# Six local-attention layers on one core: the product with V from a banded probability tile, and small VectorE steps on GpSimd or PSUM

## What is computed

```python
bk2, bv2 = (look(bk), look(bv))                 # previous window and own window
sim = jnp.einsum('bhwie,bhwje->bhwij', bq, bk2) * QK_SCALE
sim = jnp.where(mask, -jnp.finfo(sim.dtype).max, sim)
attn = jax.nn.softmax(sim, -1)
out = jnp.einsum('bhwij,bhwje->bhwie', attn, bv2)
```

## Time and profile before

| | |
|---|---|
| runs | 3551.12 us median, 3550.79 and 3555.56 the others |
| span of the profiled execution | 3553.3 us |
| time of the profiled execution | not listed by itself; one run is above its span, 3555.56 us |
| busy | TensorE 3325.9 us (94%), VectorE 2737.3 (77%), ScalarE 2545.5 (72%), GpSimd 2041.5 (57%) |
| mean granted TensorE clock | 0.984 |

### The profile page before, as it was taken

How to read it: one execution, slowest core, us unless ns; L and a number is a source line. 1 busy time by engine, 2 the same in 40 slices (tenths; PEclk the granted TensorE clock), 3 DMA queues, 4 the chain that set the end, 5 groups by cost and what they waited for, 6 DMA issues and landing times.

```text
span 3553.3 us, 149054 instructions
## 1 busy us (share of the span) xinstructions
PE 3325.9 (94%) x65032; PEld 2107.6 (59%) x65032; DVE 2737.3 (77%) x3420; ACT 2545.5 (72%) x5866; POOL 2041.5 (57%) x1557
## 2 busy tenths in 40 slices
PE   7999987999999999999999999999999999999996
PEld 3444434666666666666666666666666666666663
DVE  3656557888887878888788878788888878788883
ACT  4667655777777777777777767677777777787774
POOL 0000006766676666766666666667676667676661
PEclk9999998999999999999999999999999999999998
DMA  3223224333333333433333333334333333333330
GB/s 109 76 71 84 75 61 141 135 127 127 134 133 133 118 127 130 140 131 129 119 122 136 130 124 127 127 124 143 126 130 126 121 136 125 135 127 131 129 122 24
DMA packets 247337, 423.34 MB, mean 119 GB/s; under 512 B 71966, under 2 KB 110108, under 8 KB 246556
## 3 DMA queue, kind: packets, MB, share of 16 engines
q1 hardware_dynamic: 220368, 397.28, 33.1%
q10 hardware_dynamic: 26316, 16.52, 1.6%
HBM read 124.21 MB, written 7.34 MB: 37 GB/s over the span
## 4 chain that ended last, share of the span: by engine, by line
PE 64%; DVE 17%; issue 7%; ACT 5%; POOL 5%; DMA 1%; SPq 1%; DVEq 0%; POOLq 0%; ACTq 0%
PE PS L535 64%; DVE TPB L932 5%; DVE MX L956 2%; ACT SC L1237 1%; DVE NV L947 1%; POOL K L1324 1%; POOL Q L1342 1%; DMA RB<-root_scratch 1%; POOL K L1342 1%; DVE PP L977 1%; DVE PX L978 1%; DVE NV L945 1%; DVE H L800 1%; DVE H L1000 1%; DVE NV L949 1%
## 5 line engine op out<-in xcount | busy, mean ns | idle before, releaser
L932 DVE SCALAR_TENSOR_TENSOR TPB<-PS,VEC,C 128x1024 f32<-128x1024 f32 x768 | 961.8, 1270 | 102.0 <-ACT SX L1213 95.0
L1237 ACT ACTIVATE SC<-PS,BQ,RQ 128x64 f32<-128x64 f32 x3072 | 979.5, 436 | 40.7 <-DVE BQ L961 40.3
L1213 ACT ACTIVATE SX<-PS 128x512 f32<-128x512 f32 x768 | 461.5, 620 | 391.4 <-PE PS L535 388.4
L1324 POOL TENSOR_TENSOR K<-K,RB 128x512 f32<-128x512 f32 x384 | 497.2, 1295 | 283.1 <-DMA RB<-root_scratch 278.4
L1347 POOL TENSOR_TENSOR SC<-SC,RC 128x1024 f32<-128x1024 f32 x192 | 366.3, 1908 | 480.2 <-DVE RC L969 478.8
L535 PEld LDWEIGHTS PS<-PP,VV 32*64 32x64 f32 x24576 | 433.7, 133 | 278.6 <-issue 276.3
L535 PE MATMUL PS<-PP,VV 32*64 32x64 f32 (+1 forms) x24576 | 541.2, 223 | 7.8 <-issue 6.2
L1342 POOL TENSOR_TENSOR K<-TPB,TR 128x512 f32<-128x512 f32 x384 | 496.4, 1293 | 0.0
L1342 POOL TENSOR_TENSOR Q<-TPB,TR 128x512 f32<-128x512 f32 x384 | 495.5, 1290 | 0.0
L535 PE MATMUL PS<-LXH,LH 128*128 128x512 f32 x768 | 371.3, 484 | 85.2 <-DVE TPB L932 68.4
L535 PE MATMUL PS<-K,Q 64*32 64x64 f32 (+1 forms) x24576 | 302.2, 224 | 49.5 <-issue 48.0
(11 more groups left out here) (167 smaller groups left out, 5809.8 us busy)
## 6 DMA issues: line engine op xcount, KB each, us to landing
TR<-TPB SPq DMA_DIRECT2D x768, 256.0 KB, 2.7
RB<-root_scratch SPq DMA_DIRECT2D x768, 128.0 KB
PP<-PX SPq DMA_DIRECT2D x192, 192.0 KB, 2.6
WS<-in_wqkv ACTq DMA_DIRECT2D x72, 128.0 KB, 2.4
PP<-PX SPq DMA_DIRECT2D x192, 48.0 KB, 2.5
QA<-TH SPq DMA_DIRECT2D x128, 64.0 KB, 2.1
QA<-TL SPq DMA_DIRECT2D x128, 64.0 KB, 2.1
KA<-TH SPq DMA_DIRECT2D x128, 64.0 KB, 2.1
```

The source lines that it names most:

```text
L932: e.scalar_tensor_tensor(TPB[:, n % 3:4 + n % 2:3 + n % 2 - n % 3, w, :], g, VEC[:, l, 9 + w:10 + w], C[:, at:at + 1024].rearrange("p (o c ...
L1213: e.activation(SX[i % 3][:, :], bk("PJ", key)[:, :], ACT.Square).then_inc(sem["pj_act"], 1)
L1237: p = e.activation(SC[m % 2][:, g, :, :].rearrange("p x k -> p (x k)"), bank[s][:, at:at + 64], ACT.Exp, bias=BQ[m % 2][:, g:g + 1], scale ...
L1324: e.tensor_tensor(dst, dst, RB[n % 2][:, :], ALU.mult).then_inc(sem["pr_pool"], 1)
```

## The change

- PV has two rounds of 16 products. Each takes 64 rows (two windows) and moves 96 columns (three output windows); PP has three blocks per row, of which one in each row quarter is zero and never written again. The four products of one c are two row halves by two column halves, and all products of one row half write one bank at a time.
- TT transposes both parts into two PX tiles, and the stage PX fills PP with eight DMAs on SP's queue where there were two.
- NM2 becomes four GpSimd instructions; BQ becomes a GpSimd instruction (a stage of its own), and the maximum is negated as it is taken.
- rsqrt() keeps its intermediate and its result in the PSUM bank of the sums; F3 reads it there. The bank is held until the last reader is done.
- All of PLACE has new numbers.

```diff
-    "LS": 221.000, "LB": -1.200, "LO": -0.800, "S1": -0.074, "MX": 0.116, "S3": (0.544, 0.762, 0.998, 1.143),
-    "SU": 1.382, "NP": 1.294, "TT": 2.458, "PX": 2.427, "PV": (4.410, 5.233, 5.448, 5.789), "PVn": 6.127,
-    "PJ": (-7.620, -7.132), "PQ": (-7.575, -7.217), "PT": (-7.306, -7.188), "TS": -6.939, "SS": -6.491,
-    "AD": -5.748, "NM1": -3.351, "NM2": -3.290, "RW": -3.234, "RQ": -1.711, "RB": -2.631, "PR": -2.007,
-    "XS": -9.372, "XSl": -9.254, "VP": -0.635, "VC": -0.652, "WO": (12.673, 12.742, 12.742, 12.755),
+    "LS": 220.609, "LB": -1.007, "LO": -0.147, "S1": -0.039, "MX": 0.127, "BQ": -0.409,
+    "S3": (0.527, 0.769, 0.988, 0.821), "SU": 1.191, "NP": 1.545, "TT": 2.465, "PX": 2.765, "PV": (4.790, 5.030),
+    "PVn": 6.097, "PJ": (-7.633, -7.092), "PQ": (-7.531, -7.184), "PT": (-7.291, -7.112), "TS": -6.917, "SS": -6.304,
+    "AD": -5.801, "NM1": -3.418, "NM2": -3.856, "RW": -3.141, "RQ": -1.741, "RB": -3.132, "PR": -1.967, "XS": -9.711,
+    "XSl": -10.141, "VP": -0.635, "VC": -0.581, "WO": (12.860, 12.894, 12.955, 12.965), "F1": 13.910, "F2": 14.289,
...
-        lay(z + P["F2"], group, "F2", u, "f2_dve", 3 * u + 1)
+        lay(z + P["F2"], group, "F2", u, "f3_dve", u + 1)
...
-        PP = [sb(f"PP{i}", [128, 2, 16, 32]) for i in range(2)]
-        PX = sb("PX", [128, 16, 32])
+        PP = [sb(f"PP{i}", [128, 3, 16, 32]) for i in range(2)]
+        PX = [sb(f"PX{i}", [128, 16, 32]) for i in range(2)]
...
                 elif st == "PX":
                     m, = key
-                    a, z = PX, PP[m % 2]
+                    z = PP[m % 2]
+                    if m == 0:
+                        on.wait_ge("band_pool", 2)
                     if m > 1:
-                        on.wait_ge("pv_pe", 4 * m - 4)
+                        on.wait_ge("pv_pe", 2 * m - 2)
+                    on.wait_ge("tt_dve", 2 * m + 1)
+                    for r in range(4):
+                        k = slice(32 * r, 32 * r + 32)
+                        e.dma_start(z[k, r % 2, :, :], PX[0][k, :, :]).then_inc(sem[f"px_in{m % 2}"], 16)
                     on.wait_ge("tt_dve", 2 * m + 2)
-                    e.dma_start(z[0:96, 1, :, :], a[32:128, :, :]).then_inc(sem[f"px_in{m % 2}"], 16)
-                    e.dma_start(z[96:128, 1, :, :].rearrange("p (x c) a -> p x c a", c=4)[:, :, 0:3, :],
-                                a[0:32, :, :].rearrange("p (x c) a -> p x c a", c=4)[:, :, 1:4, :]).then_inc(sem[f"px_in{m % 2}"], 16)
+                    for r in range(1, 4):
+                        e.dma_start(z[32 * r - 32:32 * r, 1 + (r + 1) % 2, :, :],
+                                    PX[1][32 * r:32 * r + 32, :, :]).then_inc(sem[f"px_in{m % 2}"], 16)
+                    e.dma_start(z[96:128, 2, :, :].rearrange("p (x c) a -> p x c a", c=4)[:, :, 0:3, :],
+                                PX[1][0:32, :, :].rearrange("p (x c) a -> p x c a", c=4)[:, :, 1:4, :]).then_inc(sem[f"px_in{m % 2}"], 16)
...
                     else:
-                        on.wait_ge("pv_pe", 4 * p + rho)
+                        on.wait_ge("pv_pe", 2 * p + 1)
                     for c in range(4):
-                        for x in range(2):
+                        for t in range(2):
                             for s in range(2):
-                                r = (rho + 2 * x + s) % 4
-                                j = 4 * c + r
-                                w = min(2, 16 - j)
+                                x = (t + rho) % 2
+                                j = 4 * c + 2 * t
+                                w = min(3, 16 - j)
                                 h = 2 * ((2 * p + x) % 8) + s
-                                y = mm(bank[2 + x][64 * s:64 * s + 64, 32 * j:32 * j + 32 * w],
-                                       VV[32 * r:32 * r + 32, c, 64 * h:64 * h + 64],
-                                       PP[p % 2][32 * r:32 * r + 32, 0:w, 8 * s + 4 * x + c, :],
-                                       rho == 0 and c == 0, rho == 3 and c == 3, skip_group_check=True)
+                                k = slice(64 * t, 64 * t + 64)
+                                y = mm(bank[2 + x][64 * s:64 * s + 64, 32 * j:32 * j + 32 * w], VV[k, c, 64 * h:64 * h + 64],
+                                       PP[p % 2][k, 0:w, 8 * s + 4 * x + c, :], rho == 0 and c == 0, rho == 1 and c == 3,
+                                       skip_group_check=True)
...
-            def rsqrt(v, u, x, step, done, r):
+            def rsqrt(v, x, y, step, done, r):
                 on.wait_ge(step, 2 * r + 2)
-                e.scalar_tensor_tensor(u, v, EPS, x, ALU.add, ALU.mult).then_inc(sem[done], 1)
+                e.scalar_tensor_tensor(v, v, EPS, x, ALU.add, ALU.mult).then_inc(sem[done], 1)
                 on.wait_ge(done, 3 * r + 1)
-                e.scalar_tensor_tensor(u, u, -0.5, x, ALU.mult, ALU.mult).then_inc(sem[done], 1)
+                e.scalar_tensor_tensor(v, v, -0.5, x, ALU.mult, ALU.mult).then_inc(sem[done], 1)
                 on.wait_ge(done, 3 * r + 2)
-                e.scalar_tensor_tensor(x, u, 1.5, x, ALU.add, ALU.mult).then_inc(sem[done], 1)
+                e.scalar_tensor_tensor(y, v, 1.5, x, ALU.add, ALU.mult).then_inc(sem[done], 1)
...
-                    e.tensor_reduce(MX[:, :], g, AX_X, ALU.max).then_inc(sem["s1_dve"], 1)
-                    on.wait_ge("s1_dve", 2 * m + 1)
-                    if m > 1:
-                        on.wait_ge("s3_act", 4 * m - 4)
-                    on.wait_ge("rq_act", m // 2 + 1)
-                    e.scalar_tensor_tensor(BQ[m % 2][:, :], MX[:, :], -1.0, rq(m), ALU.mult, ALU.mult).then_inc(sem["s1_dve"], 1)
+                        on.wait_ge("bq_pool", m)
+                    e.tensor_reduce(MX[:, :], g, AX_X, ALU.max, negate=True).then_inc(sem["s1_dve"], 1)
...
-                    e.transpose(PP[m % 2][:, 0, :, :], SC[m % 2][:, :, 1, :]).then_inc(sem["tt_dve"], 1)
-                    e.transpose(PX[:, :, :], SC[m % 2][:, :, 0, :]).then_inc(sem["tt_dve"], 1)
+                    e.transpose(PX[0][:, :, :], SC[m % 2][:, :, 1, :]).then_inc(sem["tt_dve"], 1)
+                    e.transpose(PX[1][:, :, :], SC[m % 2][:, :, 0, :]).then_inc(sem["tt_dve"], 1)
...
-                    e.tensor_tensor(H[2][:, :], H[1][:, :], FX[:, :], ALU.mult).then_inc(sem["f3_dve"], 1)
+                    e.tensor_tensor(H[2][:, :], H[1][:, :], bk("F2", key)[:, :], ALU.mult).then_inc(sem["f3_dve"], 1)
...
+                elif st == "NM2":
+                    q, = key
+                    v, u, x = NV[:, 0, :], NV[:, 1, :], NV[:, 2, :]
+                    on.wait_ge("nm_act", 2 * q + 2)
+                    e.tensor_tensor(u, v, x, ALU.mult).then_inc(sem["nm_pool"], 1)
+                    on.wait_ge("nm_pool", 4 * q + 1)
+                    e.tensor_tensor(u, u, x, ALU.mult).then_inc(sem["nm_pool"], 1)
+                    on.wait_ge("nm_pool", 4 * q + 2)
+                    e.tensor_scalar(u, u, -0.5, 1.5, ALU.mult, ALU.add).then_inc(sem["nm_pool"], 1)
+                    on.wait_ge("nm_pool", 4 * q + 3)
+                    e.tensor_tensor(x, u, x, ALU.mult).then_inc(sem["nm_pool"], 1)
+                elif st == "BQ":
+                    m, = key
+                    if m > 1:
+                        on.wait_ge("s3_act", 4 * m - 4)
+                    on.wait_ge("rq_act", m // 2 + 1)
+                    on.wait_ge("s1_dve", m + 1)
+                    e.tensor_tensor(BQ[m % 2][:, :], MX[:, :], rq(m), ALU.mult).then_inc(sem["bq_pool"], 1)
```

More of the change, by code:

```diff
@@ L159, in squares @@
     def squares(kind, b):
-        o.put("N2", kind, b, banks=[(None, kind + "_root", 3, 1)])
-        o.keep(o.bank["N2", (kind, b), 0], kind + "_root", 3 * b + 1)
+        o.put("N2", kind, b, banks=[(None, kind + "_root", 3, 3)])
+        o.keep(o.bank["N2", (kind, b), 0], kind + "_root", 3 * b + 3)
     def norm(kind, b, z, places, at=at):
@@ L290, in order @@
             m = n // 2
-            for st in ("S1", "MX", "SU", "NP", "TT", "PX", "PVn"):
+            for st in ("S1", "MX", "BQ", "SU", "NP", "TT", "PX", "PVn"):
                 lay(n + P[st], o.put, st, m)
@@ L294, in order @@
                 lay(n + P["S3"][i], o.put, "S3", m, i)
+            for i in range(2):
                 lay(n + P["PV"][i], o.put, "PV", m, i)
@@ L386, in build @@
         H = [sb(f"H{i}", [128, L]) for i in range(3)]
-        FX = sb("FX", [128, L])
         AOf = AO[0][:, :, :].rearrange("p a b -> p (a b)")
@@ L427, in nroot @@
         def nroot(kind):
-            return EZ if kind == "end" else NZ[("in", "mid", "x").index(kind)]
+            return ES if kind == "end" else NZ[("in", "mid", "x").index(kind)]
         def nused(kind, b):
@@ L505, in sync_program @@
                             on.wait_ge(f"rb_in{n % 2}", 32 * (n // 2) + 32)
-                    on.wait_ge("nm_dve", 4 * q + 4)
+                    on.wait_ge("nm_pool", 4 * q + 4)
                     for c in range(4):
@@ L680, in tensor_program @@
```

(35 more changed lines are left out.)

6 lines of the change are left out of this document (1 added, 5 removed), and 15 rows, old and new, of the table PLACE.

## The result

The changed kernel takes 3641.26 us (median of 4 runs, 3637.81 to 3648.91) against 3552.22 for the kernel before beside it: 1.0252 times as long, 95% interval 1.0238 to 1.0267. It is slower by 89 us; 3389 was forecast. The span of the profiled execution is 3636.0 us, at a mean granted clock of 0.955 (before 0.984).

What follows compares the result with a forecast made beforehand. It took TensorE's own work as the bound, with VectorE's lateness on top. Taking 152 us for PV's rounds and 10 for waits off 3553.3 gave 3391, less 2.2 to the median: 3389 us, range 3340 to 3425.

Steps and rivals of the forecast that it cites:

- the sum: Whole kernel: 152 us saved by PV and 10 by TensorE's waits, from 3553.3 to 3391 us.
- I counted by the places, modulo two steps: TensorE's order: four blocks of small tiles per step before and after, so no second gain from tile-shape changes.
- the waits of TensorE: TensorE's idle time for VectorE: 0.05 us per step taken off, 10 us in all, of at most 0.4 per step.
- Rival A: GpSimd's in-order queue becomes the bound, its waits before NP and PR staying: 3628 us, chance 0.08.
- Rival B: PV's products that share rows don't overlap on TensorE, a round taking 1.54 us: 3664 us, chance 0.03.
- Rival C: Half the gain goes into new TensorE waits for TPB, BQ through GpSimd, or PR through SP: 3474 us, chance 0.25.
- Rival D: VectorE held TensorE up more; waits go and PV rounds hardly grow: 3325 to 3275 us, chance 0.12.

Runs made afterwards that it cites:

- e1_f4: The changed kernel with the third F4 at 16.250 instead of 16.743, ahead of the second TB; 3440.91 us, ratio 0.9701.
- e13: Kernel before with two-round PV, its eight DMAs, layer norm in SBUF and F2's bank given back early, all other places old; 3491.27 us, ratio 0.9840.
- e12: Kernel before with BQ (at -0.400) and NM2 on GpSimd, nothing else; 3544.65 us, ratio 0.9994.
- e15: Kernel before with the two DMAs of stage PX cut into eight that move the same bytes; 3564.16 us, ratio 1.0023.
- e7: Kernel before with F2's bank held until F3 has run and F3 at 14.700 instead of 15.347; 3774.88 us, ratio 1.0623.
- e6: e1_f4 with the layer norm worked out in SBUF tiles and F2's bank given back early; 3574.29 us, ratio 1.0066.
- e17: e1_f4 with PV in four rounds and its DMAs as before the change; 3718.88 us, ratio 1.0468.
- e14: e13 with BQ (at -0.400) and NM2 on GpSimd as well; 3492.63 us, ratio 0.9824.
- e18: e14 with RB at -3.132 instead of -2.631; 3533.12 us, ratio 0.9950.
- e10: e6 with F3 at 15.347, its place before the change, instead of 14.686; 3497.09 us, ratio 0.9858.
- e11: Kernel before with F3 at 14.700 instead of 15.347, nothing else; 3645.77 us, ratio 1.0274.
- e2: Kernel before with the second TB at 16.100 instead of 16.229, ahead of the third Gelu; 3991.16 us, ratio 1.1244.

## Why the prediction was wrong

**The step that failed** is in the sum: it had no term for ScalarE. I took its 11.51 us per step as given, read PLACE for the order on TensorE, GpSimd and SP ("I counted by the places, modulo two steps"), and did not read it for ScalarE, whose queue has a state, the loaded table. The kernel after has 294 more loads than before, 377 us of ScalarE's time. The place of one stage against TB, plain in the diff, was worth 200 us (e1_f4), more than the forecast gain. The forecast of 3389 plus 200 would have been 3589; the rest is 52 us by which e1_f4 too is above 3389. A second term was mis-sized, the waits of TensorE: the sum has them 0.05 us per step shorter. With the shorter rounds alone they are 0.43 us per step longer (e13, 0.75 to 1.18), in e1_f4 0.10 longer (0.85: 2357.00 us busy of 2500, 169 steps).

**Rival A** gave 3628 us and was wrong: it wanted GpSimd idle before NP and PR to stay near 4 us per step, and in the kernel after it is 58.7 / 160 = 0.37 and 4.0 / 160 = 0.03. GpSimd stands 268.1 us for MX at BQ instead; in e12 it stands 309.3 us there at no cost. That 3628 lies near the measured 3641 is luck. **Rival B** (products that share rows don't overlap) is refuted by the round itself, the timeline of TensorE after:

```profile
2006.92 0.88 PE L541 MATMUL PS<-PP,VV 64*64 64x96 f32 x32
2007.73 0.50 PE L541 MATMUL PS<-LXH,LH 128*128 128x512 f32 x1
```

0.81 us per round; 0.85 was forecast and 1.54 was B's. The Trainium skill (TensorE: Matmul & The Clock Gate, Part 3) has a weight load overlap products in flight only in another row group. Read as the prediction read it, this does not hold for these 64x64 tiles. **Rival C**'s sign was there (TensorE's idle is 1.37 us per step: 43.9 / 500 x 2500 / 160), its releaser before PJ was not: not TPB but F3. Once the loads and F3's place are out of the way, in e13, C is what the trace shows: the rounds save 0.88 us per step of TensorE's busy time, 0.43 come back as idle time, mostly for TPB, and the time is 3491 us where C had 3474. **Rival D** wanted a round under 0.7 us and waits that go away; neither came.

**What held.** The records of PV are 12288. VectorE takes 349.15 / 500 x 15.63 = 10.9 us per step (10.8 forecast), GpSimd 11.4 (11.75); its four NM2 steps and BQ are in these groups, 0.83 us per step for NM2 against 0.95 and 0.227 against 0.23 for BQ:

```profile
L1336 POOL TENSOR_TENSOR NV<-NV 128x128 f32<-128x128 f32 x80 | 36.8, 460 | 196.7 <-ACT NV L1009 196.7
...
L1340 POOL TENSOR_SCALAR NV<-NV 128x128 f32<-128x128 f32 x80 | 23.8, 298 | 7.0
...
L1349 POOL TENSOR_TENSOR BQ<-MX,RQ 128x16 f32<-128x16 f32 x160 | 36.3, 227 | 268.1 <-DVE MX L952 268.0
```

The eight issues of PX take 4.98 us (4.8 forecast), and e15 shows that the queue has room for six more issues at the old places, at about 8 us:

```profile
2052.66 2.49 SPq L527 DMA_DIRECT2D PP<-PX  x4
2055.19 1.86 SPq L530 DMA_DIRECT2D PP<-PX  x3
2057.09 0.63 SPq L532 DMA_DIRECT2D PP<-PX  x1
```

In e1_f4 a step takes 14.54 us from the first MX to the last (577.1 to 3353.5 us, 191 steps), before 15.18 (581.4 to 3480.0); 14.5 was forecast, from 15.34. That the two lie so close is in part luck, for they are of different stretches: from 900 to 3400 us, where the 15.34 comes from, e1_f4 has 169 steps, 14.79 us each, and over all steps the kernel before has 15.18. The gain per step is 0.55 in the one stretch and 0.64 in the other, 122 us in all, where the forecast had 0.84 and 162. And it is not the gain of the rounds alone, which is 56 us in e13.

**Held bank.** The prediction did not price that F2's bank is kept until F3, and named no such wait, though the diff has the line. At the old places it costs 129 us (e7); in the kernel after it is, by the waits, where the table loads reach TensorE, which no run tried by itself. In e1_f4 it still shows as 64.7 us in 40 units (900 to 3200 us), but e6, which moved the norm's operands too, was slower and not faster.

**What stays open.** The two rounds give 56 us at the old places (e13) and at most 278 at the new ones (e17). Neither VectorE's load (e14), nor SP's issues (e15), nor an earlier RB (e18) closes the gap of 52 us (44 by the ratios) between e14 and e1_f4; the two have the same work and differ in order and in where the layer norm is held. The new places alone do not bring it: e10 has them, but for F3, with e14's layer norm, and comes out as e14 does. So it comes only together with the norm in PSUM, its held bank and F3 at 14.686; these three were not taken apart at the new places. The places of PV in e13 and e14 were not varied either. The best kernel here is e1_f4, 3.0% faster than before.

## What to carry to other kernels

Where a queue's order is written out by numbers, read the new order for every engine, and for ScalarE check which table each function wants between two loads: here one Gelu behind the wrong load brought four times as many loads, and moving it back was worth 200 us. Ask for each buffer whose last reader moves who wants it next. And price a mechanism by itself before it is named as the cause: the held bank alone cost 129 us (e7 against e11), but giving it back together with a move of the norm's operands to SBUF made the kernel 133 us slower (e6), and the place of F3 alone was worth 77 to 144 us in four pairs of runs.

## What was not expected of the hardware

A table load takes 1.283 us, and here one stands before every Gelu, Ln or Exp that the loaded table lacks; Exp by itself after a Gelu brought a table without Ln, so the pair Ln, Exp, which runs with no load after TB, cost two loads per use. 386 such loads, 495 us, cost 440 us with ScalarE busy for only 77% of the time (e2): an engine's idle share hid little of them. The mean granted clock was 0.984 before, 0.955 in the kernel after and 0.935 in e2. It does not follow TensorE's busy share alone: e11 and e6 are both busy for 92% of the span, at 0.978 and 0.950. At a lower mean clock the same records were busy for longer: 65 us between e1_f4 and the kernel after, 177 between the kernel before and e2.
